# Two attention stages: projections rounded one step later, the next batch's layernorm in eight pieces

## What is computed

```python
x = x + L0_xattn(layernorm(x), ctx, ...)   # 16 heads of 64, low-rank terms, 4 image tokens of their own: stage A
x = x + L0_ffn(layernorm(x), ...)          # mixture of 8 experts, 2 for each row: stage M
x = x + L1_xattn(layernorm(x), ctx, ...)   # 8 heads of 64: stage C
x = x + L1_ffn(layernorm(x), ...)          # gated, with rounded weights: stage F

def attention(q_in, k_in, v_in):
    s = einsum('bhid,bhjd->bhij', q, k) * SCALE
    p = softmax(s)
    return einsum('bhij,bhjd->bhid', p, v)
```

## Time and profile before

| | us |
|---|---|
| median of three runs | 1023.07 |
| lowest and highest | 1023.05, 1027.87 |
| the profiled execution | 1026.1 |
| its span in the profile | 1024.2 |
| stage A, its 128 steps (62.97 to about 461.8) | 399 |
| stage C, its 64 steps (707.39 to about 916.7) | 209 |
| mean granted PE clock over the span | 0.914 of 2.4 GHz |

### The profile page before, as it was taken

The page is one execution under the profiler, slowest core; times in us unless marked ns, Lnnn a source line. Parts: engine busy times, 40 slices in busy tenths (PEclk is TensorE's granted clock), DMA queues, the critical chain, the costliest instruction groups (busy, mean ns, idle before and its releaser), DMA issues. The chain is left out here.

```text
span 1024.2 us, 23424 instructions
## 1 busy us (share of the span) xinstructions
PE 824.4 (80%) x8736; PEld 506.2 (49%) x8808; DVE 756.2 (74%) x1541; ACT 709.8 (69%) x1179; POOL 627.7 (61%) x574
## 2 busy tenths in 40 slices
PE   3788799999999999997434999967777869875676
PEld 3534465556555656565122676622444536554243
DVE  3857888778877887775686455548979878876797
ACT  3269799889988999991441444436787877991574
POOL 1059677877787778780455666433686857872443
PEclk9989899999999999996666999989898999996799
DMA  8749999999999999993883988972999998990265
GB/s 212 235 80 159 173 178 185 173 167 180 178 184 170 178 172 168 175 178 62 204 292 70 182 187 181 165 243 47 185 169 192 234 203 134 189 171 16 39 116 134
DMA packets 504878, 167.96 MB, mean 164 GB/s; under 512 B 477728, under 2 KB 495328, under 8 KB 504736
## 3 DMA queue, kind: packets, MB, share of 16 engines
q1 hardware_dynamic: 501024, 156.25, 82.5%
q0 software_dynamic: 3744, 10.23, 3.5%
HBM read 37.04 MB, written 11.14 MB: 47 GB/s over the span
## 5 line engine op out<-in xcount | busy, mean ns | idle before, releaser
L521 POOL TENSOR_TENSOR A_PHL<-A_pr,A_PHL 128x508 f16<-128x508 f32 x256 | 294.0, 1154 | 92.1 <-ACT A_pr L802 91.7
L801 ACT ACTIVATE A_PHL<-A_ps,A_negmax 128x508 f16<-128x508 f32 x256 | 190.1, 743 | 14.5 <-DVE A_negmax L1051 12.8
L802 ACT ACTIVATE A_pr<-A_ps,A_negmax 128x508 f32<-128x508 f32 x256 | 191.8, 749 | 0.0
L521 POOL TENSOR_TENSOR C_PHL<-C_pr,C_PHL 128x512 f16<-128x512 f32 x128 | 149.7, 1177 | 58.0 <-ACT C_pr L802 57.8
L1051 DVE TENSOR_REDUCE A_negmax<-A_ps 128x2 f32<-128x1016 f32 x128 | 154.3, 1206 | 0.0
L647 PE MATMUL A_ps<-A_K,A_Q 64*128 64x512 f16 x768 | 106.5, 383 | 18.0 <-ACT A_pr L802 13.9
L665 PE MATMUL A_ps<-A_VH,A_PT 128*128 128x65 bf16 (+1 forms) x1024 | 108.1, 196 | 7.7 <-DMA A_PT<-A_PHL 7.7
L666 PE MATMUL A_ps<-A_VL,A_PT 128*128 128x64 f16 (+1 forms) x1024 | 108.1, 193 | 0.0
L667 PE MATMUL A_ps<-A_VH,A_PT 128*128 128x65 bf16 (+1 forms) x1024 | 108.0, 194 | 0.0
L665 PEld LDWEIGHTS A_ps<-A_VH,A_PT 128*128 128x128 f16 (+1 forms) x1024 | 94.8, 98 | 22.2 <-DMA A_PT<-A_PHL 10.7
L801 ACT ACTIVATE C_PHL<-C_ps,C_negmax 128x512 f16<-128x512 f32 x128 | 89.6, 700 | 20.2 <-DVE C_negmax L1051 17.8
(11 more groups left out here) (342 smaller groups left out, 2286.4 us busy)
## 6 DMA issues: line engine op xcount, KB each, us to landing
A_PT<-A_PHL SPq DMA_TRANSPOSE x256, 3.4
M_raw<-in_L_ffn_w_in SPq DMA_DIRECT2D x4, 1024.0 KB, 8.1
M_raw<-in_L_ffn_w_out SPq DMA_DIRECT2D x4, 1024.0 KB, 9.2
C_yc<-routed_rows SPq DMA_DIRECT2D x8, 512.0 KB, 5.1
M_rows<-M_xhl SPq DMA_DIRECT2D x4, 512.0 KB, 9.1
out<-X SPq DMA_DIRECT2D x16, 128.0 KB, 2.1
X<-in_x SPq DMA_DIRECT2D x1, 1536.0 KB, 14.0
ct_split<-A_CT SPq DMA_DIRECT2D x4, 384.0 KB, 3.0
```

Of the source, the lines that this page charges most:

```text
L521: pool.tensor_tensor(PHL[:, e % PRING, 1, 0:KEYS], pr[:, e % RING, 0:KEYS], PHL[:, e % PRING, 0, 0:KEYS], ALU.subtract).then_inc(pl_ready. ...
L801: a.activation(PHL[:, e % PRING, 0, 0:KEYS], o, ACT.Exp, bias=nm[:, n % 4, h:h + 1])
L802: a.activation(pr[:, e % RING, 0:KEYS], o, ACT.Exp, bias=nm[:, n % 4, h:h + 1]).then_inc(p_ready.sem, 1)
```

## The change

`at` is sorted inside each step so that `q`, `k` and `v` come last. If the last job of a step is one of these and the next step has fewer than two jobs, it becomes "late" (`late_of`), all others are "early". PE runs all jobs where it did, apart from the sorting. ACT writes the high half of a late job of step g-1 in step g, behind `weights(g-1)`, where it was written in step g-1 ahead of them. DVE writes its low half in step g behind the maximum of step g, where it stood ahead of it.

```diff
+    early, late_of = {}, {}
+    for step in sorted(at):
+        at[step].sort(key=lambda u: u[0] in "qkv")
+        spread = at[step][-1][0] in "qkv" and len(at.get(step + 1, [])) < 2
+        early[step] = at[step][:-1] if spread else at[step]
+        late_of[step] = at[step][-1:] if spread else []
@@ ScalarE
                 if 1 <= g <= G:
                     weights(g - 1)
-                for u in at.get(g, []):
+                for u in late_of.get(g - 1, []) + early.get(g, []):
                     if u[0] in HI_KINDS:
                         high(u)
@@ VectorE
             for g in range(G + TAIL + 1):
-                for u in at.get(g - 1, []):
+                for u in early.get(g - 1, []):
                     low(u)
```

```diff
+    SPREAD = 15 if ipa else 0
-    SUM_AT = (40, 42, 44, 46, 50, 52)
-    SCALE_AT = 55
+    SUM_AT = (46, 48, 50, 52, 56, 58)
+    SCALE_AT = 61
@@ VectorE, behind the maximum of step g
-                    if ipa and nb < B and g % U in (10, 12, 14):
-                        if g == 10:
+                for u in late_of.get(g - 1, []):
+                    low(u)
+                if g < G:
+                    t0, k = nb * QT, g % U - SPREAD
+                    if nb < B and 0 <= k < 8 and (ipa or nb > 1):
+                        if ipa and g == SPREAD:
                             wait(v, x_rest, 16)
-                        normal(nb * QT, (nb + 1) * QT, (g % U - 10) // 2)
+                        if k < 2:
+                            normal(t0 + 2 * k, t0 + 2 * k + 2, 0)
+                        if k == 2:
+                            normal(t0, t0 + QT, 1)
+                        if k in (2, 3):
+                            newton(t0, t0 + QT, k - 1)
+                        if k >= 4:
+                            normalise_x(nb, k - 4, k - 3)
-                        if nb < B and u in (4, 5, 6):
-                            normal(nb * QT, (nb + 1) * QT, u - 4)
-                    if g % U == U - 9 and nb < B:
-                        normalise_x(nb)
+                        if nb == 1 and u in (4, 5, 6):
+                            normal(QT, 2 * QT, u - 4)
+                        if nb == 1 and u in (7, 8):
+                            normalise_x(1, 2 * u - 14, 2 * u - 12)
```

More of the change, by code:

```diff
@@ L894, in lower, with normalise_x @@
                                 hi[:, :, :].rearrange("p c n -> p (c n)"), ALU.subtract).then_inc(w_split.sem, 1)
-            def normalise_x(b):
-                if ipa and b:
+            def normalise_x(b, t0=0, t1=QT):
+                if ipa and b and t0 == 0:
                     wait(v, ct_split, 2 * b + 2)
-                for t in range(QT):
+                for t in range(t0, t1):
                     n = b * QT + t
@@ L902, in normalise_x @@
                                            ALU.subtract, ALU.mult)
-                last.then_inc(xn_ready.sem, 1)
+                if t1 == QT:
+                    last.then_inc(xn_ready.sem, 1)
             def low(u):
@@ L970, in normal @@
                 if part == 0 and not ipa:
-                    wait(v, mixed, t1 // QT * 2)
+                    wait(v, mixed, -(-t1 // QT) * 2)
                 if part == 0:
@@ L984, in normal, with newton @@
                 if part == 2:
-                    for _ in range(3):
-                        ln.link(v.tensor_tensor(two, y, y, ALU.mult))
-                        ln.link(v.tensor_tensor(one, two, half_v, ALU.mult))
-                        ln.link(v.scalar_tensor_tensor(out=y, in0=one, scalar=1.5, in1=y, op0=ALU.add, op1=ALU.mult))
+                    newton(t0, t1, 3)
+            def newton(t0, t1, rounds):
+                one, two, half_v = [stats[k][:, t0:t1] for k in ("ve", "sd", "tmp")] if ipa else [a[:, t0:t1] for a in lt]
+                y = stats["rstd"][:, t0:t1]
+                for _ in range(rounds):
+                    ln.link(v.tensor_tensor(two, y, y, ALU.mult))
+                    ln.link(v.tensor_tensor(one, two, half_v, ALU.mult))
+                    ln.link(v.scalar_tensor_tensor(out=y, in0=one, scalar=1.5, in1=y, op0=ALU.add, op1=ALU.mult))
             ln = Chain(v, ln_links)
```

## The result

The changed kernel took 1056.28 us (median of three runs, 1055.89 to 1058.08) against 1023.07. The changed kernel is slower by 33 us; the prediction said 9, with a range up to 1042. The sign was right, the size was not, and the time lies outside the range.

What follows compares the result with a forecast made beforehand. PE was taken to bound A's second and third batches. The terms, -10 + 15 + 1 - 1 + 4.8 + 2.4 - 3 = +9.2 us, added to 1023.1, gave 1032 us, with a range of 1010 to 1042.

Steps and rivals of the forecast that it cites:

- Term 4: Late K halves delay the scores in A and C: +4.8 us at eight light places, +2.4 at eight beside `v`.
- Term 6: At step 24 the sorting puts `o` ahead of `q`: 0.4 us, counted within the layernorm's gain, so nothing extra.
- Term 1: The layernorm leaves steps 10 to 14 and 23 of A: -7 us in the first batch, -1.5 each in two, -10.
- Term 2: Layernorm in A's steps 15 to 22, its small operations meeting POOL's subtractions: +5 us for each of three batches, +15.
- the free 2.7 and the crowded 8.3: Us for the 13 small operations of A's steps 17 and 18, without and with POOL's subtractions running back to back.
- The 20 us that I named for that case: If each of A's 13 small operations waited for a full subtraction, 15 us a batch, the sum would be 20 higher.
- Term 3: Layernorm moved to steps 2 and 3 in C: +1 us in its second batch, -1 in its third.
- Term 5: Q's wait for PE goes: 1.75 us at step 4 of A's first batch, 1.2 in C's first batch, -3 together.
- (a): Rival, chance 0.22: small operations fall into POOL's rests and late K halves find slack; faster by 8 us, 1010 to 1015.
- (b): Rival, chance 0.25: gains and costs cancel across the kernel, +1 us, so 1024, with 1019 to 1028 around it.
- (c): Rival, chance 0.08: stalls pull PE's clock in A's second and third batches down to 0.95; +10 us, 1042.
- 7 or more: Sign of being right: PE's idle time in A's second and third batches rises from 3.5 us to at least 7.

## Why the prediction was wrong, and where it was right

The steps that failed are terms 4 and 6: the price of the late halves, which was counted for K alone and for too few places, and that of the sort, which was put at nothing. Within A the runs make a ladder: before 396.6; pieces 395.7; DVE's low halves behind the maximum, with the part of the sort that leaves `i` alone, 400.9 (+5.2); ACT's high halves behind the exponentials 414.0 (+13.1); the sort that moves `i` 420.3 (+6.3). The drops of the clock are in these rungs. The first rung was predicted as +5, the other three in A as little more than nothing (2.4 for K beside `v`, a few places of term 4 at 0.6, -1.75 for Q). The last batch, in which no layernorm stands, can be taken apart with the drops by themselves: +0.1, +1.2 and +2.9 (95.87 in the kernel with `i` back that has no drop there), then 1.5 for the transposes and 3.1 for two drops, 8.8 together.

**Term 1 (layernorm leaves steps 10 to 14 and 23, -10): right, a little too small.** In the kernel with the pieces alone steps 10 to 15 of the first batch took 17.2 us for 23.5: -6.3, part of it a clock that no longer drops there. In the second, steps 10 to 15 won 1.5, as said, and steps 23 to 25 1.15 more. -12 in all.

**Term 2 (small operations in steps 17 and 18, +15): mechanism right, size too large.** With the pieces alone steps 17 and 18 of the second and third batch took 9.4 us for 5.5 (+3.9), and the first batch lost 3 in steps 16 to 22: +11. In the whole change the two steps took 5.40 and 4.41 us for 2.75 and 2.74; I had said 2.9 and 1.6 more, and it was 2.65 and 1.67. That these agree so well is partly luck: with the pieces alone, where no low half of V stands between, it was 3.1 and 0.8. One chain of the changed kernel, a row of POOL and three of DVE:

```profile
224.00 2.30 POOL L528 TENSOR_TENSOR A_PHL<-A_pr,A_PHL 128x508 f16<-128x508 f32 x2 [0.59 <-ACT A_pr L809]
...
224.00 0.17 DVE L990 TENSOR_SCALAR gate<-ln_ve 128x4 int32<-128x4 int32 x1
224.19 1.00 DVE L991 TENSOR_SCALAR ln_rstd<-gate 128x4 int32<-128x4 int32 x1
225.23 1.09 DVE L999 TENSOR_TENSOR gate<-ln_rstd 128x4 f32<-128x4 f32 x1
```

Two of the first seven meet a subtraction, 1.0 and 1.1 us, one of the last six does (1.05 at 229.52), and the 13 take 5.1 us, between the free 2.7 and the crowded 8.3. Taken at its worst, the rule of the Trainium skill that I had weighed (SBUF — State Buffer, Who interferes with whom: who comes first has the shared ports for the whole instruction) would have every one of them wait for a whole subtraction, 15 us. The trace agrees with the exclusion and not with that sum, since POOL rests when DVE is late (3.10 us ahead of 229.40). The 20 us that I named for that case are counted from the crowded price, 3 times 15 less 8.3, and not from my own sum, as I wrote.

**Term 3 (C): second batch right, third mis-sized.** With the pieces alone the second batch took 53.9 for 53.0 (+1 predicted, +0.9 measured). The third took 53.3 us, for 58.6 and 60.7 in two traces of the kernel before: -5 to -7 where I had -1. I counted only the 2.6 us that PE waited for `o` and not that the lump of `xn` and sum held up the next maxima too.

**Term 4 (K late, +7.2): right at the place where it was worked out, wrong as a sum.** The chain of 2.27, 3.0 and 3.75 us came as said, up to the start of the scores. The two steps from 456.30 took 6.40 us for 5.84 before (from 435.07 to 440.91 there, both from the timeline of ACT), but the clock drops inside them; in the kernel with `i` back that has no drop there they took 5.89, and the four steps 12.15 us for 11.88, +0.3 for a priced 0.6. Where `y` stands it costs nothing, as said: in A's last batch, of the whole change with `i` back, steps 8 to 15 take 0.4 us more than with ACT's rounding early. C's first batch grew by 1.6 us and its last by 2.6, four places each. What failed is the count. PE now waits for K's low half 18 times in A and 12 times in C, where I had priced 16 places in all. I asked of the late halves only who waits for K. I never asked it of V, whose half is late in the same way: it cost A 12 us alone, since the image softmax, the first weighing of a head half and V's next projection stand behind it. And I took each place by itself, while a low half that comes late joins whatever DVE has next (steps 14 and 15 in the kernel with K alone late).

**Term 5 (Q, -3): right in sum, elsewhere in part.** Q alone late gave 0.9956, some -4.6 us, but A's steps are only 0.2 us shorter than before, where I had put 1.75, and C's 7, where I had put 1.2. The sum is right partly by luck.

**Term 6 (the sort, 0): wrong.** I read it for `o` and `q` at step 24 and did not look at what else it reorders. At step 3 it puts `i`, which waits for a chain of ACT and DVE, ahead of `v`, which waits for nothing. 6 us in A by the step lengths, in both pairs of kernels that differ by it, about half of it the wait and half the clock.

**The rivals.** (a), that all is faster, has its sign in the pieces alone, but not its mechanism: the 13 did not fall into POOL's rests, and the overrun of steps 17 and 18 was 3.9 us, not 2.1. (b) fell. (c), that stalls pull the clock down, holds in kind: A's last three batches fell from 1.00 to 0.98, 0.98 and 0.97, not to 0.95, at an estimated 6 us where I had put 10, and stage M has its part, where I had not looked for one. By itself it explains neither the waits nor the time. What the prediction said would show it right did so: PE's idle time rose from 3.5 to 10 us, the 13 took 5.1 us, and the scores of C wait for K, 24.2 us in 12 waits. It said "7 or more" and had no bound above, which was the fault of the whole sum: its unknowns were bounded at the places counted, not by the number of places. One sign that it named spoke against it: A's first batch, which was to shrink by 2 us or more, went from 101.83 only to 101.30. Terms 1 and 2 are not at fault there, since with the pieces alone it is 98.37; the late halves took the rest.

## What to carry to other kernels

When a result's rounding is moved behind other work, list every reader of that result, on every engine, and what stands behind each reader in its own order. In these runs the price was set there, and a late half cost most where it joined other work. Moving by kind helped only for the kind with slack (Q, wanted two steps later than K). The half that lay behind four exponentials cost about two and a half times the one behind a maximum, in all of A (13.1 and 5.2 us) and in the last batch (2.9 and 1.2). A sort that "only" reorders equals has to be read at each place where it changes something: one job that waits, put ahead of one that doesn't, cost 6 us of A here, the clock included. And before a step's growth is priced as a wait, its granted clock has to be read.

## What the runs showed of the hardware

An operation of 4 columns on DVE takes 0.16 us alone and mostly 1.0 to 1.2 us when it meets one of POOL's subtractions of 1.15 us. Which of the two is a matter of the moment: of the first seven, five and four met one in two batches of the kernel with the pieces at step 8, and two in the changed kernel.

In the same kernel, at the same step and behind the same idle time of PE (2.28 and 2.27 us), the granted clock dropped to 1.2 GHz in one trace and not in the other, and the two steps took 8.60 or 7.18 us. So equal instructions can differ by 1.4 us, and batch lengths that repeat to 0.02 us do so where the drops repeat.

The first 70 us behind A's last exponentials run at a mean granted clock of 0.57 to 0.65, which moves the whole kernel by 2 to 4 us, as much as some of the effects looked for here.
